# Second segments of a selective scan: the carried state enters through ScalarE instead of as the scan's initial value

## What is computed

```python
def _selective_scan(u, delta, A, B, C, D):
    deltaA = jnp.exp(jnp.einsum('bld,dn->bldn', delta, A))
    deltaBu = jnp.einsum('bld,bln,bld->bldn', delta, B, u)
    def step(h, inputs):
        dA_t, dBu_t, C_t = inputs
        h = h * dA_t + dBu_t
        y = jnp.einsum('bdn,bn->bd', h, C_t)
        return (h, y)
    ...
    return y + u * D
```

## Time and profile before

| | |
|---|---|
| median of 3 runs | 1881.86 us (1879.46 to 1888.6) |
| the profiled execution | 1884.71 us |
| its span, first to last instruction | 1883.0 us |
| busy: PE, DVE, POOL, ACT | 1613.8, 1205.5, 1128.1, 790.8 us |
| segments 0, 1, 2, 3 begin scanning at | 82.7, 316.7, 555.0, 793.6 us |
| last scan begins | 1008.8 us |

### The profile page before, as it was taken

One profiled execution on the slowest core, in us unless ns is written; L12 is line 12 of the kernel. 1 busy time (PEld: TensorE's weight loads), 2 busy tenths in 40 slices (PEclk: granted clock), 3 DMA queues, 4 the chain that ended last, 5 costly groups with the idle time before them and its releaser, 6 DMA issues. The chain is left out here.

```text
span 1883.0 us, 18250 instructions
## 1 busy us (share of the span) xinstructions
PE 1613.8 (86%) x4198; PEld 726.3 (39%) x4199; DVE 1205.5 (64%) x1707; ACT 790.8 (42%) x1287; POOL 1128.1 (60%) x695
## 2 busy tenths in 40 slices
PE   5679998999988999898779599992599999999995
PEld 2233433444333444333333254551244444444442
DVE  3599999999999999899994233317532333333331
ACT  4466576665766666566562243410011111111110
POOL 0199899998889988999985111100144444544443
PEclk9889999999999999999999799996699999999998
DMA  3600125101151110410000621210167676676663
GB/s 111 264 18 23 38 65 200 35 33 39 54 209 37 31 36 26 181 43 25 7 17 12 246 85 61 67 39 17 33 150 214 176 198 187 173 196 185 155 145 57
DMA packets 65360, 182.86 MB, mean 97 GB/s; under 512 B 10016, under 2 KB 14368, under 8 KB 56608
## 3 DMA queue, kind: packets, MB, share of 16 engines
q1 hardware_dynamic: 47232, 138.48, 20.8%
q0 software_dynamic: 18080, 43.82, 11.9%
HBM read 147.65 MB, written 34.62 MB: 97 GB/s over the span
## 5 line engine op out<-in xcount | busy, mean ns | idle before, releaser
L753 POOL TENSOR_TENSOR h<-h,c_rep 128x2048 f32<-128x2048 f32 x128 | 579.0, 4527 | 29.9 <-DVE h L656 24.9
L846 PE MATMUL bank<-h,ident 128*128 128x512 f32 x916 | 444.7, 628 | 88.9 <-POOL h L753 68.7
L500 ACT ACTIVATE bank<-delta,a_neg 128x512 f32<-128x512 f32 x512 | 335.8, 681 | 167.2 <-DVE h L656 166.5
L846 PEld LDWEIGHTS bank<-h,ident 128*128 128x128 f32 x916 | 178.3, 199 | 332.6 <-issue 212.9
L656 DVE TENSOR_TENSOR_SCAN h<-bank,state,h 128x512 f32<-128x512 f32 x256 | 305.9, 1259 | 0.5 <-ACT bank L500 0.5
L656 DVE TENSOR_TENSOR_SCAN h<-bank,h 128x512 f32<-128x512 f32 x256 | 290.6, 1199 | 1.4 <-ACT bank L500 1.4
L1573 PE MATMUL h_ps<-w_ring,xT 128*128 x640 | 285.4, 599 | 3.5 <-issue 3.4
L646 DVE TENSOR_TENSOR h<-bank,b_rep 128x2048 f32<-128x2048 f32 (+1 forms) x105 | 227.4, 2184 | 45.1 <-ACT bank L493 31.3
L1524 DVE TENSOR_TENSOR act<-gs,h_ps 128x256 f32<-128x256 f32 x80 | 33.7, 421 | 248.4 <-ACT gs L1497 248.4
L1497 ACT ACTIVATE gs<-h_ps 128x256 f32<-128x256 f32 x80 | 30.7, 384 | 379.6 <-PE h_ps L1573 379.6
L1573 PEld LDWEIGHTS h_ps<-w_ring,xT 128*128 128x128 f32 x640 | 120.8, 191 | 163.3 <-issue 163.3
(11 more groups left out here) (214 smaller groups left out, 1835.9 us busy)
## 6 DMA issues: line engine op xcount, KB each, us to landing
w_ring<-in_w SPq DMA_DIRECT2D x32, 1024.0 KB, 6.2
b_rep<-bcd SPq DMA_DIRECT2D x16, 1024.0 KB, 6.9
c_rep<-bcd SPq DMA_DIRECT2D x16, 1024.0 KB, 4.9
w_ring<-in_w SPq DMA_DIRECT2D x32, 512.0 KB, 8.4
w_in<-in_w_in_x SPq DMA_DIRECT2D x32, 256.0 KB, 2.6
w_res<-in_w_in_res SPq DMA_DIRECT2D x32, 256.0 KB, 2.7
xa<-in_x SPq DMA_DIRECT2D x20, 256.0 KB, 3.0
xb<-in_x SPq DMA_DIRECT2D x16, 256.0 KB, 2.7
```

The costliest lines, as they stand in the source:

```text
L500: eng.activation(da[j][:], delta[:, g % 2], ACT.Exp, scale=a_neg[:, col:col + 1])\
L753: ins = eng.tensor_tensor(h[:, q], h[:, q], c_rep[:, Q * q:Q * q + Q, :], ALU.mult)
L846: ins = eng.matmul(y_ps[:], c.ident[:], h[:, q, j, :], start=False, stop=(q == NQ - 1 and j == Q - 1))
```

## The change

In segments 1 and 3 the scans start from 0.0. Before each such scan ScalarE replaces the first column of the B product in place, by first + da[:, 0] * state: one activation (Identity) of 128x1 that reads the first column of the decay from PSUM, takes the state column as its scale and the first column of the product as its bias. The scan then waits for this operation (semaphore `carried`) and no longer for the decay itself. The carry of state j is queued behind the decay of state j + 1, the last one behind its own decay. The first carry of a quarter also waits for the quarter's B product, whoever makes it.

```diff
--- before.py
+++ after.py
@@ -133,7 +133,7 @@
                  "rvar_ready ms_ready rrms_ready scales_ready pool_chain xn_ready tap_done "
                  "conv_chain xs_ready bcd_written sp_chain sp_ready delta_ready "
                  "du_made du_ready bq_made b3_made da_ready scan_done state_saved weighed cmul_done y_summed gate_done "
-                 "xr_ready").split()
+                 "xr_ready carried").split()
         S = {n: sem("m_" + n) for n in names}
         b_loaded = [sem(f"m_b_loaded{q}") for q in range(NQ)]
         c_loaded = [sem(f"m_c_loaded{q}") for q in range(NQ)]
@@ -191,6 +191,11 @@
         def folded(g, q):
 
             return leaving(g) and q < NQ - 1
+
+        def carried_before(g):
+
+            s, d = divmod(g, DC)
+            return (s // 2 * DC + d) * NS
 
         def after(eng, s, n):
             if n > 0:
@@ -492,13 +497,28 @@
                         eng.wait_ge(S["bq_made"], v_count[g - 1, NQ - 1])
                     eng.activation(du_ps[:], du[:], ACT.Copy).then_inc(S["du_ready"], 1)
 
+                def carry(g, q, j):
+
+                    col = (g % DC) * NS + q * Q + j
+                    if j == 0:
+                        spread_done(eng, g, q)
+                    eng.wait_ge(S["da_ready"], (g * NQ + q) * Q + j + 1)
+                    first = h[:, q, j, 0:1]
+                    eng.activation(first, da[j][:, 0:1], ACT.Identity, scale=state[:, col:col + 1], bias=first)\
+                        .then_inc(S["carried"], 1)
+
                 def decay(g, q):
+                    later = g // DC % 2 == 1
                     for j in range(Q):
                         n = (g * NQ + q) * Q + j
                         after(eng, S["scan_done"], n - Q + 1)
                         col = (g % DC) * NS + q * Q + j
                         eng.activation(da[j][:], delta[:, g % 2], ACT.Exp, scale=a_neg[:, col:col + 1])\
                             .then_inc(S["da_ready"], 1)
+                        if later and j > 0:
+                            carry(g, q, j - 1)
+                    if later:
+                        carry(g, q, Q - 1)
 
                 eng.wait_ge(S["small_loaded"], NSM)
                 eng.activation(a_neg[:], a_neg[:], ACT.Exp).then_inc(S["aneg_ready"], 1)
@@ -650,10 +670,11 @@
                     s, d = divmod(g, DC)
                     spread_done(eng, g, q)
                     for j in range(Q):
-                        eng.wait_ge(S["da_ready"], (g * NQ + q) * Q + j + 1)
-                        col = d * NS + q * Q + j
-                        init = 0.0 if s % 2 == 0 else state[:, col:col + 1]
-                        eng.tensor_tensor_scan(h[:, q, j, :], da[j][:], h[:, q, j, :], init, ALU.mult, ALU.add)\
+                        if s % 2 == 0:
+                            eng.wait_ge(S["da_ready"], (g * NQ + q) * Q + j + 1)
+                        else:
+                            eng.wait_ge(S["carried"], carried_before(g) + q * Q + j + 1)
+                        eng.tensor_tensor_scan(h[:, q, j, :], da[j][:], h[:, q, j, :], 0.0, ALU.mult, ALU.add)\
                             .then_inc(S["scan_done"], 1)
 
                 def gate(g):
```

## The result

| | before | changed |
|---|---|---|
| median of 15 runs (lowest to highest) | 1883.29 us (1879.46 to 1888.6) | 1890.47 us (1885.11 to 1894.92) |
| ratio, 95% interval | | 1.0037 (1.0024 to 1.0049) |
| span of the profiled execution | 1883.0 us | 1887.8 us |

The change costs 7.2 us, 0.37%. It is clear of noise and within the 0.5% that the prediction calls no change. The forecast was 1884 in 1873 to 1895.

What follows compares the result with a forecast made beforehand. VectorE was taken to set the pace in segments 1 and 3, GpSimd close behind. Terms -5.7 + 5.9 + 1.4 = +1.6 us gave 1883.5 on the median's terms, written as 1884, range 1873 to 1895.

Steps and rivals of the forecast that it cites:

- the rival in which the scans do not get shorter: The 60 ns have another source than the state column; no gain, stalls remain: about 1891, chance 0.04.
- The removed 60 ns: Segments 1 and 3: 256 scans go from 1259 to 1199 ns, at most 15.4 us of VectorE.
- The price of a carry: ScalarE: each of 256 one-column operations takes 0.36 us, 0.29 us of the queue when behind a decay.
- Place 1: Start of chunks 12 and 13: carries waiting for the B product delay tap and convolution, 5.9 us together.
- Place 2: Quarters 2 and 3 of chunks 12 and 13: scans wait for late carries, net loss 0.7 each, 1.4 us.
- Place 3: Quarter 3 of chunks 15 and 26 to 30: in chunk 28 carry 0.3 late, 0.5 with faster scans, in existing idle.
- Chunks 8, 9, 10, 24, 25 ... 0.5 each: Shorter scans save 0.96 us each, but GpSimd is close behind VectorE, so 0.5 each, 2.5 us.
- Chunks 11 and 26 ... 0.2 and 0.3: GpSimd is full in these chunks, so shorter scans gain only 0.2 and 0.3, together 0.5 us.
- the removal: Shorter scans in segments 1 and 3: 5.7 us gained over the chunks, without chunks 12 and 13.
- the addition: Loss from carries in ScalarE's queue: 5.9 us at Place 1 and net 1.4 us at Place 2.
- the whole saving arrives: Rival: carries follow decays more cheaply and GpSimd's chunks shorten with VectorE's; up to 15.4 us, 1866.5, chance 0.09.
- the carry breaks the run of decays: Rival: carries cannot overlap decays and cost 0.55 us or more of ScalarE's queue; 14 us above forecast, 1898, chance 0.17.

Runs made afterwards that it cites:

- e1: Changed kernel with the waiting tap queued ahead of quarter 0's four carries at the start of chunks 12 and 13: 1886.35 us, ratio 1.0012.
- e7: Changed kernel plus two zero-matrix matmuls on PE ahead of its wait for quarter 2 of chunks 9 and 25: 1890.55 us, ratio 1.0038.
- e9: Kernel before with GpSimd's addition L758 cut to one column: 1875.57 us, ratio 0.9953.
- e2: Changed kernel without any carries, all scans starting from 0.0 and the state left out: 1882.18 us, ratio 0.9994 to the kernel before.
- e10: e2 with GpSimd's addition L758 cut to one column: 1863.99 us, ratio 0.9893 to the kernel before.
- e3: Changed kernel with carries writing a scratch column and scans starting from the state column again: 1893.09 us, ratio 1.0053.
- e5: Changed kernel with each carry directly behind its own decay: 1889.2 us, ratio 1.0038.

## Why the prediction was right, and what was off in it

The time lay 6.5 us over the forecast and inside the range; the verdict of no change by the 0.5% bound was right. Part of this is luck. The forecast of the change itself was +1.6 us and it measured +7.2, near the upper end of the forecast's own range (1891), and 7.2 is not far under the bound of 9.4. The nearest single number in the prediction is that of the rival in which the scans do not get shorter, 1891, and its mechanism is false: they did.

- *The removed 60 ns.* Right: 1259 to 1200 ns, four scans in 4.56 us.
- *The price of a carry.* Right: 341 ns against 0.36 us. A decay begins 0.25 us after the carry ahead of it, where I had 0.29, and the next carry 0.61 us after that (429.77, 430.02, 430.63 in the timeline above).
- *Place 1, "2.5 us" and "3.4 us".* Right: convolution at 432.77 against 432.65, idle 3.04 us twice, 0.79 and 0 before; 5.3 us in all against 5.9. e1 took 4.5 of them back.
- *Place 2, "a net loss of 0.7 each".* Right: idle 1.54 before quarter 2 (I had 1.2), chunk 13 +0.7 us; chunk 12 +3.8, which is the tap's 3.0 and 0.7.
- *Place 3, covered or 0.5 us.* In chunk 15 the size was wrong: it lost 1.3 us where I had a gain of 0.24, and VectorE waits 1.25 us for the carry before quarter 3, where I had 0.3 to 0.5. Chunk 27 gained 0.3 (0.5), chunks 28 to 30 together 1.1 (0.72); but in e7, with the same carries there, these three took 83.4 us as before (83.5), so this last agreement proves nothing.
- *"Chunks 8, 9, 10, 24, 25 ... 0.5 each", "Chunks 11 and 26 ... 0.2 and 0.3".* This is the step that failed. It gives a gain of 1.5 us to chunks 8 to 10, and of 1.3 to chunks 24 to 26. Measured, the two groups of three lost 0.7 and 0.1: 84.6 became 85.3 us, and 85.2 became 85.3. The price of GpSimd was not far off: where no fall of the clock came into the group, as in e1 and e7, chunks 8 to 10 took 83.6 us, a gain of 1.0; GpSimd's own 27.7 us three times over are 83.1. What the prediction lacked is the chain behind GpSimd (its addition, PE's sum, `xb` and the decays in ScalarE's queue) and the fall of PE's clock in it. This fall costs 1.7 us in chunk 10; in the kernel before the clock fell in chunk 9 (346.4, the 0.94 of the earlier trace rows), and the chunk took the same 28.2 us as in e9, so that chunk hid it. In e2, with no carry on ScalarE, chunk 10 still lost 1.8. With GpSimd relieved (e10 against e9) the three chunks gain 3.0.

  Which of the three chunks pays is not fixed: it is 10 and 26 in the changed kernel and e2, 25 in e1 and e7. The lengths of single chunks are from one execution of each kernel. The prediction's own sign of being wrong, chunks 8 to 10 shorter by the full 0.96 us, came true for 8 and 9 and not for 10.

In the sum, then, with the 1.4 us that place 2 takes off for shorter scans (0.24 and 0.48 in each of two chunks) counted as removal: I had put the removal at 7.1 us, and it measured 2.6 (changed kernel against e3) or 1.3 (e2 against before); I had put the addition at 8.7 us, and e3 measured 9.6. The addition was about right, the removal nearly three times too large. The rival "the whole saving arrives" fell in e2; it needs a GpSimd that has room, which e10 gave it. The rival "the carry breaks the run of decays" needed 0.5 us in the queue per carry, and a decay begins 0.24 to 0.25 us after the carry ahead of it. In e5, where each carry waits for its own decay, a small part of it is real: the convolution of chunk 12 waits 0.95 us longer.

By the Trainium skill (ScalarE: Activation LUTs, "What ACT_TABLE_LOAD costs") a carry is estimated at 373 ns, of which 280 ns count in the queue; the runs show 341 and about 240, so its figures are a little high here. The Trainium skill's tip (ScalarE: Activation LUTs, "Step-by-step: what each stage is for") that ScalarE writes PSUM faster than SBUF was dismissed in the prediction by two copies of 600 and 601 ns. These differ in what they read as well as in what they write. A row that reads SBUF, as the 600 ns copy does, but writes SBUF, stands in the groups of the kernel before:

```profile
L462 ACT ACTIVATE xs<-xs 128x512 f32<-128x512 f32 x32 | 18.3, 620 | 2.3 <-DVE xs L625 2.2
```

That is another function (SiLU) and 20 ns more, so the trace does not speak against the tip. The carry came out cheaper than its price all the same (341 ns against 0.36 us), and nothing in the sum hangs on it.

What stays open: why chunk 15 ends later even without carries (e2: 28.9 us against 28.4), how much of the 7.2 us is in the clock's falls, whose place differs between executions (one profile of each kernel can't tell), and what sets off a fall.

## What to carry to other kernels

An operation added to an engine with a third of its time free can still cost, if it waits for another engine: ask what stands behind the wait in that queue, and who waits for that. Here carries of 0.34 us put 3 us in front of a tap, and moving the tap ahead of them took most of that away. Before the busiest engine is relieved, look at the second busiest over several steps in a row, because a saving that it can't follow is handed back a step or two later. And before a difference between two traces is put down to an edit, look for a third run that lacks the edit and shows the same.

## What the runs showed of the hardware

A one-column activation behind a full one takes little of the queue: 341 ns long, but the next decay begins 0.24 us after it. A scan of 128x512 takes 1200 ns from a constant and 1259 ns from a state column. After a stretch in which PE was busy 0.33 of 2.6 us its clock fell to half for 3.4 us in one execution (changed kernel) and stayed at 1.00 in another with the same stretch (e1). The fall cost 1.7 us in chunk 10, and nothing in chunk 9 of the kernel before. Two matmuls put into the stretch left the time of the kernel where it was (1890.55 against 1890.47 us).
